# Group-norm attention on one core: the per-image rows of mean, scale and bias made earlier in the slot, the next image's mean and the last one's denominators later

## What is computed

```python
xn = group_norm(x, gamma, beta)          # 8 groups of 8 channels, over all 1024 pixels
xf = xn.reshape(B, 1024, 64)
q, k, v = xf @ wq + bq, xf @ wk + bk, xf @ wv + bv
attn = softmax(einsum('bnc,bmc->bnm', q, k) * 64 ** -0.5)
out = einsum('bnm,bmc->bnc', attn, v) @ wp + bp
return xf + out
```

## Time and profile before

| | us |
|---|---|
| median of 3 runs | 193.72 |
| lowest and highest of them | 193.47, 194.7 |
| the profiled execution, its time | 193.27 |
| the profiled execution, span from first to last instruction | 191.5 |
| busy in the span: PE, POOL, DVE, ACT | 185.4, 142.2, 134.3, 112.9 |

### The profile page before, as it was taken

The page is one execution under the profiler, slowest core; times in us unless marked ns, Lnnn a source line. Parts: engine busy times, 40 slices in busy tenths (PEclk is TensorE's granted clock), DMA queues, the critical chain, the costliest instruction groups (busy, mean ns, idle before and its releaser), DMA issues.

```text
span 191.5 us, 3343 instructions
## 1 busy us (share of the span) xinstructions
PE 185.4 (97%) x1246; PEld 97.3 (51%) x1246; DVE 134.3 (70%) x179; ACT 112.9 (59%) x185; POOL 142.2 (74%) x92
## 2 busy tenths in 40 slices
PE   7989899999999999999999999999999999999994
PEld 7655455344643755355643655355542745444452
DVE  3599766876797856878586856868587847719763
ACT  3594787669645665569645665468545655248620
POOL 4168595999999899995999599995999599950000
PEclk9999999999999999999999999999999999999999
DMA  5596000000000000001000010001000000001002
GB/s 152 185 397 229 0 0 0 5 2 2 0 3 0 28 30 3 0 2 58 0 0 0 19 41 2 0 5 55 0 0 5 24 32 0 0 5 55 3 18 91
DMA packets 4415, 6.95 MB, mean 36 GB/s; under 512 B 832, under 2 KB 1456, under 8 KB 4400
## 3 DMA queue, kind: packets, MB, share of 16 engines
q1 hardware_dynamic: 4400, 6.75, 10.1%
HBM read 4.59 MB, written 2.10 MB: 35 GB/s over the span
## 4 chain that ended last, share of the span: by engine, by line
PE 87%; DMA 5%; DVE 3%; SPq 2%; issue 1%; DVEq 0%
PE attn L875 28%; PE scores L817 26%; PE wide L788 12%; DMA values<-in_x_dram 3%; PE misc L911 3%; PE scores L772 3%; PE scores L778 3%; PE misc L895 2%; DMA max_rows<-max_T 2%; PE misc L759 2%; PE misc L902 1%; DVE chunk_max L609 1%; PE misc L803 1%; PE misc L917 1%; DVE y_out L737 1%
## 5 line engine op out<-in xcount | busy, mean ns | idle before, releaser
L320 POOL TENSOR_TENSOR prob_sum<-prob_sum,probs 128x1024 f32<-128x1024 f32 x42 | 100.7, 2397 | 5.9
L609 DVE TENSOR_REDUCE chunk_max<-wide 128x1 f32<-128x1024 f32 x60 | 73.3, 1222 | 31.2 <-PE wide L788 30.6
L421 ACT ACTIVATE probs<-scores 128x1024 f32<-128x1024 f32 x64 | 63.4, 1022 | 30.0 <-PE scores L817 29.0
L875 PE MATMUL attn<-probs,values 128*64 128x512 f32 x248 | 60.0, 605 | 0.0
L788 PE MATMUL wide<-k_hi,q_hi 64*128 64x512 f32 x120 | 30.7, 472 | 1.2 <-DVE chunk_max L609 1.0
L875 PEld LDWEIGHTS attn<-probs,values 128*64 128x64 f32 x248 | 15.0, 136 | 25.5 <-issue 23.1
L320 POOL TENSOR_TENSOR prob_sum<-probs 128x1024 f32<-128x1024 f32 x7 | 16.6, 2376 | 11.3 <-ACT probs L421 11.3
L788 PEld LDWEIGHTS wide<-k_hi,q_hi 64*128 64x128 f32 x120 | 12.5, 183 | 22.0 <-DVE chunk_max L609 12.3
L817 PE MATMUL scores<-q_hi,step_hi 64*128 64x512 f32 x96 | 20.8, 426 | 0.3
L817 PE MATMUL scores<-q_lo,step_hi 64*128 64x512 f32 x96 | 19.3, 390 | 0.0
L817 PE MATMUL scores<-q_hi,step_lo 64*128 64x512 f32 x96 | 19.2, 390 | 0.0
(11 more groups left out here) (151 smaller groups left out, 240.5 us busy)
## 6 DMA issues: line engine op xcount, KB each, us to landing
x_T<-in_x_turned_dram SPq DMA_DIRECT2D x8, 256.0 KB, 6.8
values<-in_x_dram SPq DMA_DIRECT2D x8, 256.0 KB, 6.9
out_dram<-y_out SPq DMA_DIRECT2D x7, 256.0 KB, 2.1
out_dram<-y_out SPq DMA_DIRECT2D x2, 128.0 KB, 1.7
max_rows<-max_T SPq DMA_DIRECT2D x14, 4.0 KB
packed<-in_packed_dram SPq DMA_DIRECT2D x1, 192.0 KB, 3.8
packed<-in_packed_dram SPq DMA_DIRECT2D x1, 130.5 KB, 2.6
bp_all<-in_bp_dram SPq DMA_DIRECT2D x1, 32.0 KB, 4.5
```

The lines of the kernel that those rows point to most:

```text
L320: nc.gpsimd.tensor_tensor(prob_sum[b % 2][:, :], so_far[:, :], probs[i][:, :], ALU.add).then_inc(sum_done, 1)
L421: nc.scalar.activation(probs[i][:, :], scores[flip_of(b, i)][:, :], ACT.Exp, scale=SCALE).then_inc(exp_done, 1)
L609: nc.vector.reduce_max(chunk_max[:, p, j:j + 1], made_in[:, :], AX.X).then_inc(max_done, 1)
L875: product = nc.tensor.matmul(attn[x_half * C:(x_half + 1) * C, :], values[b][:, t * C:(t + 1) * C], probs[i][:, x_half * HALF:(x_half + 1) ...
```

## The change

The order of the work in a slot changes; no instruction is added or taken away. Slot 0 keeps its order.

- PE: `rows_of(p)` moves from between score tile 5 and chunk 4 to behind chunk 1, ahead of score tile 2. Its wait for `y_done` (for `misc` to be empty) comes with it. `group_mean(z)` and `denominators(b-1)` move from behind `weigh_values(b, 1)` to behind `weigh_values(b, 3)` and wait for `add_bias(p)`; `turn_denominators` moves from behind chunk 4 to behind chunk 6. Slot 6, written out apart, changes alike.
- ACT: `gain_of(s)` moves from behind exponential 2 to ahead of exponential 0. `copy_mean(z)` and `copy_den(b-1)` move from ahead of exponential 4 to ahead of exponential 6, `sum_squares(z)` from behind exponential 4 to behind exponential 6.
- DVE: `normalise(s)` moves from behind maximum 2 to ahead of maximum 1; `centre`, `scale` and `add_bias` follow maxima 1, 2 and 3 instead of 4, 5 and 6; `invert` follows maximum 6 instead of 4.

The diff, without the repetition of it in slot 6:

```diff
@@ scalar
                 if b > 0:
                     copy_attn(b - 1)
+                if b > 0 and exists(s):
+                    gain_of(s)
                 exp_tile(b, 0)
                 exp_tile(b, 1)
...
                 if b == 0:
                     sum_turned(z)
-                elif exists(s):
-                    gain_of(s)
                 exp_tile(b, 3)
...
-                if exists(z):
                     copy_mean(z)
                 if b == LAST:
                     scale_w_vp(b - 1)
-                if b > 0:
                     copy_den(b - 1, misc)
                 exp_tile(b, 4)
-                if exists(z):
+                if b == 0:
                     sum_squares(z)
...
                 if 0 < b < LAST:
                     scale_w_vp(b - 1)
+                    if exists(z):
+                        copy_mean(z)
+                    copy_den(b - 1, misc)
                 exp_tile(b, 6)
+                if b > 0 and exists(z):
+                    sum_squares(z)
@@ vector
-                    if s >= 2:
-                        dve.wait_ge(den_turned, s - 1)
...
-                reduce_chunk(p, 1, wide)
-                reduce_chunk(p, 2, wide)
                 if b > 0 and exists(s):
                     normalise(s)
+                reduce_chunk(p, 1, wide)
+                if b > 0:
+                    centre(p)
+                reduce_chunk(p, 2, wide)
+                if b == 1:
+                    scale(0)
+                if b > 0:
+                    scale(p)
                 reduce_chunk(p, 3, wide)
+                if b == 1:
+                    add_bias(0)
+                if b > 0:
+                    add_bias(p)
                 reduce_chunk(p, 4, wide)
...
@@ tensor
                 next_max_chunk(p, 1)
+                if b == 1:
+                    pe.wait_ge(var_eps_done, 4)
+                    pe.wait_ge(maxT_copied, 1)
+                elif b > 1:
+                    pe.wait_ge(y_done, b - 1)
+                if b > 0:
+                    pe.wait_ge(gain_done, p)
+                    rows_of(p)
                 next_tile(b, 2)
                 next_tile(b, 3)
...
                 weigh_values(b, 2)
                 weigh_values(b, 3)
+                if b > 0:
+                    pe.wait_ge(residual_done, residuals_up_to(p))
+                    if exists(z):
+                        pe.wait_ge(sum_T_done, z)
+                        group_mean(z, misc[:, 2 * P:2 * P + 1])
+                    pe.wait_ge(sum_done, SUMS * b)
+                    denominators(b - 1, prob_sum[(b - 1) % 2], misc)
                 next_max_chunk(p, 5)
                 next_tile(b, 6)
                 next_tile(b, 7)
                 next_max_chunk(p, 6)
+                if b > 0:
+                    turn_denominators(b - 1, misc)
```

More of the change, by code:

```diff
@@ L701, in _ @@
                     add_eps(2, misc[:, 0:1])
-                if b > 0:
-                    invert(b - 1, misc)
[L704 to L712, removed]
+                    centre(p)
+                reduce_chunk(p, 5, wide)
+                if b == 0:
+                    scale(p)
+                reduce_chunk(p, 6, wide)
+                if b == 0:
+                    add_bias(p)
+                else:
+                    invert(b - 1, misc)
                 reduce_chunk(p, 7, wide)
@@ L1015, in _ @@
                     pe.wait_ge(q_lo_done, 2)
[L1016 to L1021, removed]
                     pe.wait_ge(sum_T_done, 2)
                     group_mean(2, misc[:, 2 * P + 1:2 * P + 2])
[L1024 to L1029, removed]
+                    pe.wait_ge(sum_T_done, 3)
+                    group_mean(3, misc[:, 2 * P:2 * P + 1])
                 next_max_chunk(p, 3)
@@ L1032, in _ @@
                 next_tile(b, 5)
-                if exists(z):
-                    pe.wait_ge(mean_done, z - 1)
                 if b == 0:
+                    pe.wait_ge(mean_done, 2)
                     pe.wait_ge(bias_out_done, 1)
[L1037 to L1040, removed]
+                    pe.wait_ge(gain_done, 1)
+                    rows_of(1)
                 next_max_chunk(p, 4)
@@ L1044, in _ @@
                     group_variance(2, misc[:, 0:1])
-                if b > 0:
-                    turn_denominators(b - 1, misc)
                 weigh_values(b, 2)
                 weigh_values(b, 3)
+                if b > 0:
[5 more added lines that the diff above has]
+                    denominators(b - 1, prob_sum[(b - 1) % 2], misc)
                 next_max_chunk(p, 5)
@@ L1089, in _ @@
             weigh_values(b, 1)
-            pe.wait_ge(y_done, b - 1)
-            pe.wait_ge(sum_done, SUMS * b)
-            denominators(b - 1, prob_sum[(b - 1) % 2], misc)
             next_max_chunk(p, 3)
```

## The result

| | before | changed |
|---|---|---|
| median of 4 runs, us | 193.59 | 197.35 |
| lowest and highest | 193.34, 194.7 | 196.38, 198.43 |
| profiled execution: time, span | 193.27, 191.5 | 197.83, 196.0 |
| its mean granted clock | 1.000 | 0.983 |

The ratio is 1.0165, with a 95% interval of 1.0118 to 1.0211. I had said 194.7 and at most 196.2: the change costs 3.76 us between the medians where I forecast 1.0, nearly four times as much. (In the profiled executions of e1, e2, e6, e7 and e9 the prologue takes 7 to 9 us longer; the comparisons leave such executions out, and of these five only the lengths of the slots and their rows are used.)

The account below looks back on a forecast made before the run. PE, busy for 97% of the span, was taken as the bound. Slot 1 at +2.0 and five later slots at -0.20 each gave +1.0 on 193.72, so 194.7 us, range 193.1 to 196.2.

Parts of the forecast that it names:

- The gap in slot 1: Slot 1: the early gain waits for POOL's root, exponential 0 comes 2.62 us later; with rows and scalings +2.0.
- -0.8 for the rows: Slot 1, PE: the eight row matmuls lie wholly in the stall and leave their old place, saving 0.8 us.
- +0.2 for the two scalings: Slot 1, DVE: scalings for images 0 and 2 between maxima 2 and 3 delay the chunks, 0.2 us.
- rival (C): Slot 1, PE: the clock falls in the stall and costs about 2 us more, 196.7 in all; chance 0.07.
- The steady slots: Slots 2 to 6: moving the rows changes each slot by 0.30 - 0.50 = -0.20 us, five slots -1.0.
- The old place: Slots 2 to 6, PE between tile 5 and chunk 4: taking the rows away gains 0.50 us net.
- The new place: Slots 2 to 6, PE between chunk 1 and tile 2: rows wait for `finish`, chunk 2 comes 0.30 us later.
- nothing at all, if the restart costs another 0.2: Slots 2 to 6: bound of no gain per slot, if PE's restart behind `finish` takes 0.2 us more.
- The stall doesn't return: Slots after slot 1: POOL's root is ready before exponential 0, with a margin of 0.5 us or more.
- What was to cost nothing: Slots 2 to 6: moved mean, denominators and sum of squares take their time along, at no cost.

Follow-up runs that it names:

- e1: Changed kernel with the gain of slot 1 back behind exponential 2 and its normalisation behind maximum 2: ratio 1.0046, 194.56 us at full clock.
- e2: Kernel before with one line moved, in slot 1 the gain of image 3 ahead of exponential 0: ratio 1.0221, 196.07 us at full clock.
- e6: e4 with finish ahead of maximum 0 on DVE: ratio 1.0115 to the kernel before, 195.51 us at full clock.
- e7: Changed kernel with slot 1 in the whole order of the kernel before, slots 2 to 6 left changed: ratio 0.9973, 193.49 us at full clock.
- e9: e4 with the normalisation of image 3 in slot 1 behind maximum 4: ratio 1.0007 to the kernel before, 193.69 us at full clock.
- e10: The changed kernel itself, run again for its spread: ratio 1.0100 to the kernel before, 195.13 us at full clock (one execution).
- e3: Changed kernel with seven products of unused result ahead of the rows of slot 1: ratio 1.0082 to the kernel before, 195.29 us at full clock.
- e4: Changed kernel with image 3's root on POOL behind the fifth of slot 0's seven sums, not the last: ratio 1.0026, 193.70 us at full clock.
- e11: Changed kernel with three products of unused result ahead of the rows of slot 1: ratio 1.0067 to the kernel before, 195.47 us at full clock.

## Why the prediction was wrong

**The gap in slot 1 (+2.0): right, in place and size.** Exponential 0 at 45.53, tile 3 at 47.54 and chunk 2 at 48.34 were forecast. e10, whose prologue runs as before, has 45.55, 47.53 and 48.33, and the slot is 1.93 longer. By its chunks, chunk 1 to chunk 2 takes 4.68 instead of 2.09, which is +2.59 for the 2.62 forecast, and chunk 3 to chunk 4 takes 1.85 instead of 2.53, -0.68 where I had -0.8 for the rows and +0.2 for the two scalings. The scalings cost next to nothing (1.85 against 1.82 in slot 3), so those two terms were each off by 0.1 to 0.2 and made up for each other. Bringing the root forward gives back only 1.57 (e3 less e4), because in e4 the normalisation runs beside POOL's sum and holds up chunk 2, while in e10 it ends at 46.98 and maximum 1 behind it at 48.11, ahead of chunk 2. I had counted it at 0.54 in slot 1 too, though the timeline of DVE in the kernel before shows more there:

```profile
47.30 2.02 DVE L565 TENSOR_SCALAR xn<-x_T,minus_mean,gain_col 128x512 f32<-128x512 f32 x1
```

**The clock, rival (C): this is the step that failed and took the time out of the range.** The sum put it at nothing. I priced it at 2 us and gave it a chance of 0.07, with the argument that no stretch of the trace shows a comparable idle time, which speaks neither way. It cost 1.36 in slot 1 (25.59 less 24.23), less than the price because the clock is low from 48.3 to 51.6 and not for 4.5 us (my reading of the earlier trace rows as the lower level holds: those products start 0.21 apart up to 5.2 and 0.11 apart behind 11.5, though the windows give a granted clock of 1.00 for both), and it comes in about two executions of three. Without a fall the changed kernel takes 195.13, inside the range; with one it takes 196.6, outside it. The Trainium skill, "TensorE: Matmul & The Clock Gate", section "HAM oscillation — how this bites in real kernels", tells of a kernel whose TensorE goes back to the lower clock in its idle gaps between bursts. The waits of its example are longer than the gap here, and the runs show the same at 1.8 us: in the profiled executions of e2 and of the changed kernel the clock falls at the gap, in e3, with the gap filled, it doesn't. I named the rule and set it aside.

**The steady slots (-0.20 each): the second step that failed, 0.0 measured.** The old place gave the 0.50 that was forecast (2.32 to 1.82). The new place costs 0.47 instead of 0.30: the rows start when forecast, 0.40 behind chunk 1, but take 0.69 behind a wait (92.12 to 92.81) where they took 0.59 in a running stream, and the two tiles behind them 1.47 rather than 1.40. e6, without the wait, has the 0.59 again (95.53 to 96.12) and the two tiles at 1.48, so the other 0.07 isn't the wait's, and its cause stays open. The bound "nothing at all, if the restart costs another 0.2" was the right value. With it the sum would have been +2.0, and with the clock +3.4. The 3.76 between the medians holds the second falls of two of the four executions as well, told of below.

**The spread of the kernel before: overlooked.** In 44% of its executions the clock falls once and adds 1.2 us; where, no trace of it shows, but the changed kernel's has one in the prologue that both share. Of the changed kernel's first four runs two had a second fall. So the median of four, 197.35, lies about 0.7 above the 196.6 that one fall alone gives. Full clock against full clock the change costs 1.5 us (195.13 from a single execution), one fall against none 3.0.

**The stall doesn't return**: right. Slots 2 to 5 show no wait of ACT for the root; slots 2 to 4 are 21.59 or 21.60 and slot 5 is 21.48, for 21.45 before. What was to cost nothing (mean, denominators, squares) cost 0.04: in slot 3 chunk 2 to chunk 3 is 0.63 shorter without them, and chunks 4 to 5 and 6 to 7 are 0.29 and 0.38 longer.

## What to carry to other kernels

When a small instruction moves ahead in a strictly ordered queue, look up its producer in every pass of the loop: in the first pass the producer may be a whole pass later than in the others, and then everything behind the small instruction waits for it. A gap of 2 us on a TensorE that is otherwise full cost its length here and, in most executions, the clock behind it; where such a gap can't be closed, try a few products whose results nobody uses in it. Work that is put into a gap saves only what the gap leaves after the restart, so count the restart of both.

## What the hardware did that I had not expected

- A gap of about 2 us in a stream that was 94% busy just before was followed by half clock from 48.3 to 51.6, though work resumed at 48.05. It cost 1.36 to 1.40. With 0.81 us left empty (e11) the profiled execution kept its clock, and so did six of the other seven.
- A normalisation of 128x512 on DVE (one tensor read, two scalars per partition) took 0.54 while POOL was idle, and 1.29 (changed), 1.62 (e1), 1.86 (e9), 2.02 (before, slot 1) or 2.76 (e4) when it met a POOL instruction. It then ended 0.28 or 0.29 behind the end of that instruction, or in the changed kernel of the second of two that follow each other at once; in e4 the sum had even begun 0.08 after it (42.81 against 42.73). The 128x1024 maxima beside the same sums keep their 1.22, and `centre`, which reads one tensor from `misc` in PSUM, its 0.67 (e4, at 46.54). It goes the other way too. In slot 3 of the kernel before the normalisation begins at 90.74, in the last 0.02 of a sum, and keeps its 0.54; the next sum, beside its second half, takes 2.62 instead of 2.38:

```profile
90.90 2.62 POOL L320 TENSOR_TENSOR prob_sum<-prob_sum,probs 128x1024 f32<-128x1024 f32 x1
```

  The Trainium skill, "SBUF — State Buffer", section "Who interferes with whom", describes this as one pair of ports that DVE in its two-port modes and GpSimd hold for a whole instruction, whichever comes first. The ends seen here fit that, and no run here varied the form of the normalisation to prove it.
- The kernel before, full as PE is in it, has a fall of the clock in 25 of 57 executions, worth 1.2 us, which is more than the change costs in slots 2 to 6 together.
